# A decoder of two layers on one core: other places for the maximum products, the full-row products and the key scaling in a cross attention

## The chip, the cores and the metric

The kernel runs on one core of a Trainium2 chip. The metric is the device time in microseconds (us) of one execution. The engines are TensorE (PE: matrix products; PEld is its weight load), VectorE (DVE), ScalarE (ACT), GpSimd (POOL) and the DMA queues. They run side by side, each in its own program order, and wait for one another on semaphores. TensorE writes to PSUM, eight banks of 128 x 512 float32; the other tiles lie in SBUF.

## What is computed

A decoder of two layers, each with an attention, a cross attention and a feed-forward part. The change lies in the cross attention of layer 0, and at its seam to the recurrence that follows it. Cut to these:

```
B, S, D, HEADS, DH = 2, 1024, 256, 4, 64          # latents: 2 x 1024 tokens; context: 2 x 64 of width 192
ln = layernorm(latents); xn = layernorm(ctx)
q = ln @ Wq.T
kv = concatenate([xn @ Wkv.T, ln @ Wlkv.T], axis=1)     # 64 context keys and 1024 latent keys
q, k = rmsnorm(q) * SCALE, rmsnorm(k)                   # per head
attn = softmax(where(mask, q @ k.T, -max)); out = (attn @ v) @ Wo.T + bo
x = x + out
# recurrence over the 2 batches: f, i = sigmoid(..), g = tanh(..); c = f * c + i * g; h = tanh(x wo + c uo + bo)
x = x + ffn(layernorm(x))
```

## The kernel before

All of it is `cross_attention_and_recurrence`. The attention loop has `STEPS` = 8 steps. A step n is one batch, one half of the queries (512) and one pair of heads (`part_of`); it has `GROUPS` = 9 slots kt: eight groups of 128 latent keys, and the 64 context keys. TensorE works two slots at a time. Per slot, `scores` makes two products of 64 rows (one per head of the pair) behind two small ones that add the negative maximum ("shift"); ScalarE's `exps` takes the exponential; `values` multiplies it with V, one slot behind; GpSimd adds the slots' exponentials up in `pool_sum` (the denominator), which `add_up` sums over partitions once a step; VectorE inverts it in four quarters (`invert`) and multiplies (`normalise`).

The shift of step n+1 has to be known before its scores. For it, step n makes eight maximum products, `piece(n+1, i)` in bf16. VectorE reduces each (`reduce`), then in `split_shift` joins them in four small instructions (maximum, minimum with the context's, cast to bf16, rest); TensorE turns the result (`turn_shift`) and VectorE copies it (`keep_shift`).

One tile of two PSUM banks, `ring_tile`, holds in turn every piece, turned shift, context score (`ctx`), projection (`project`), and the mean and variance of the next layer norm. TensorE's `tile(what)` waits until VectorE has read the tile before. Which of these stand at which place is written out by hand: `tiles_at(where, slot)` with the table `PIECES_AT`. "before" stands ahead of the slot's scores, "after" behind the scores of the pair and ahead of its values. VectorE walks through the same places in its own loop and reads the tiles in the same order; between them it inverts (`INVERT_AT`), normalises, scales the queries and keys of batch 1 (`scale(1, i)`, eight tiles, in step 0) and normalises tokens. GpSimd rounds these eight tiles to bf16 (`round_tile`) at the start of step 1.

Behind the loop stand the last denominator (`add_up(7)`), the last projection, and `gate_products(b, j, m)`: three gates for each block of 512 tokens, six products each (and four with the cell's state in batch 1). The first six gates take turns in two banks, and ScalarE's `gate_values` must have read a bank before it is written again. Between them lie the layer norm of the last two token blocks (`mean`, `square`, `variance`, `roots`, `normalise_tokens`) and ScalarE's high part of the tokens, `split_x(ch)`.

Of the kernel before, what the change touches and what calls it, by code (L numbers as in the profile page):

```python
# [810 lines left out]
def cross_attention_and_recurrence(nc, c):  # L811
# [6 lines left out]
    STEPS = B * NCH * FT  # L818
# [16 lines left out]
    PIECES_AT = ((("before", 0), ("before", 1), ("after", 1), ("before", 2), ("after", 3), ("before", 4), ("after", 5), ("before", 6)),  # L835
                 (("before", 0), ("after", 0), ("before", 1), ("after", 2), ("before", 3), ("before", 4), ("before", 5), ("after", 6)))

    def tiles_at(where, slot):
        n, kt = divmod(slot, GROUPS)
        odd = n % 2  # L840
        tiles = []
        if n + 1 < STEPS:
            tiles += [("piece", n + 1, i) for i, at in enumerate(PIECES_AT[odd]) if at == (where, kt)]
        if n in (1, 2) and (where, kt) == ("before", 7):
            tiles.append(("ctx", 1, n - 1))
        if n >= 2 and not odd and (where, kt) == ("after", 7):
            tiles.append(("project", n - 1))
        if n >= 3 and odd and (where, kt) == ("after", 4):
            tiles.append(("mean", (n - 3) // 2))
        if n >= 3 and odd and (where, kt) == ("before", 7):  # L850
            tiles.append(("var", (n - 3) // 2))
        if n + 1 < STEPS and (where, kt) == ("after" if odd else "before", 8):
            tiles.append(("shift", n + 1))
        return tiles
# [3 lines left out]
    for slot in range(SLOTS):  # L858
        order += tiles_at("before", slot) + tiles_at("after", slot)
# [4 lines left out]
    with ExitStack() as ctx:  # L864
# [73 lines left out]
        QUARTERS = 4  # L938
# [31 lines left out]
        with nc.Block() as block:  # L970
# [9 lines left out]
            def _(pool):  # L980
# [20 lines left out]
                for n in range(STEPS):  # L1001
                    if n == 1:
                        pool.wait_ge(*s["scaled"](16))
                        for i in range(8):
                            round_tile(1, i)
                    if n >= 2:
                        pool.wait_ge(*s["den"](n - 1))
                    for kt in range(1, POOLED if n == STEPS - 1 else GROUPS):
                        slot = GROUPS * n + kt
# [15 lines left out]
            def _(pe):  # L1025
# [283 lines left out]
                for first in range(0, SLOTS, 2):  # L1309
# [8 lines left out]
                    for slot in range(valued, upto + 1):  # L1318
                        values(slot)
                    valued = upto + 1  # L1320
# [4 lines left out]
                add_up(STEPS - 1)  # L1325
                pe.wait_ge(*left["w", OF_TOKENS[-1]](1))
                gate_products(0, 0, 0)
                project(STEPS - 1)
                gate_products(0, 0, 1)
                pe.wait_ge(*s["read"](len(order)))  # L1330
                mean(fn, 3)
                gate_products(0, 1, 0)
                variance(fn, 3)
                gate_products(0, 1, 1)
# [18 lines left out]
            def _(act):  # L1353
# [134 lines left out]
                gate_values(0, 0, 1)  # L1488
                square(fn, 3, squares(3), fn["cent"](1))
                gate_values(0, 1, 0)  # L1490
# [15 lines left out]
            def _(dve):  # L1506
# [213 lines left out]
                def empty(what):  # L1720
# [13 lines left out]
                    else:  # L1734
                        early_norm(what)

                INVERT_AT = ({("before", 2): (0, 1), ("after", 3): (2, 3)},
                             {("before", 3): (0,), ("before", 4): (1,), ("after", 4): (2,), ("before", 5): (3,)})
                NORMALISE_AT = (("before", 4), ("before", 5))
                for slot in range(SLOTS):  # L1740
                    n, kt = divmod(slot, GROUPS)
                    for where in ("before", "after"):
                        for what in tiles_at(where, slot):
                            empty(what)
                        if n >= 1:
                            for i in INVERT_AT[n % 2].get((where, kt), ()):
                                invert(n - 1, i)
                            if NORMALISE_AT[n % 2] == (where, kt):
                                normalise(n - 1)
                    if n == 0 and kt < 8:  # L1750
                        scale(1, kt)
                    if n == STEPS - 1 and kt > POOLED + 1:
                        add(slot - 1)
                    if n == 6 and kt in (5, 7):
                        normalise_tokens(fn, kt // 2 - 2)
# [2045 lines left out]
```

## Time and profile before

| | |
|---|---|
| time, median of 3 runs | 1538.76 us (1535.29 to 1540.15) |
| the profiled execution | 1539.81 us, its span 1538.0 us |
| granted TensorE clock, mean | 0.981 |
| PE busy | 1435.8 us, 93% of the span |
| DVE, ACT, POOL busy | 984.7, 752.3, 579.7 us |
| attention loop, from the first scores to the last values | some 313 to 535 us of the span |

A row of the profile names a line of the kernel, the engine, what it writes and reads, the shape and a count. In a timeline a row begins with its start and its length, both in us; the length of several merged instructions is that of all. In brackets stands how long the engine was idle ahead of it, and whom it waited for. Times of the trace are counted from the span's start.

### The profile page before, as it was taken

To read this page: it belongs to the slowest core of one execution; us is meant where nothing else is said; L and a number is where in the kernel's file an instruction comes from. 1 tells how busy PE (TensorE), PEld (TensorE's weight loads), DVE (VectorE), ACT (ScalarE), POOL (GpSimd) and SP (SyncE) were. 2 spreads that over 40 slices of the span, in tenths; PEclk is the share of its full clock that TensorE was granted. 3 is DMA by queue.
4 is the path that set the end of the run, shared out by engine and by line. 5 is a ranking of instruction groups with operands and counts; after the bars stand their busy time and mean duration, and the time that the engine had idled before them with its cause. 6 is when DMAs were issued, how large, how long until landed. Compare 5 with 4: busy or idle time off the path is not lost. (4 is left out here: it accounts for less than half of the span.)

```text
span 1538.0 us, 19014 instructions
## 1 busy us (share of the span) xinstructions
PE 1435.8 (93%) x6886; PEld 847.3 (55%) x6886; DVE 984.7 (64%) x1502; ACT 752.3 (49%) x1237; POOL 579.7 (38%) x445
## 2 busy tenths in 40 slices
PE   6999999989899899888999999798989999999998
PEld 3757764433232266453444443323668888888886
DVE  5775243888778643558888883676677575664853
ACT  4566344533345452543666665434655545445442
POOL 0035430167667610342111112202136555555552
PEclk9999999999999999998999999999999999999999
DMA  7000000000000000083435200000313223223201
GB/s 294 1 0 0 0 1 4 0 1 1 0 0 1 1 0 0 1 164 43 125 57 70 42 2 1 4 1 7 131 42 110 76 76 101 78 81 99 74 10 55
DMA packets 39044, 67.54 MB, mean 44 GB/s; under 512 B 3944, under 2 KB 19368, under 8 KB 38568
## 3 DMA queue, kind: packets, MB, share of 16 engines
q1 hardware_dynamic: 38952, 66.33, 16.2%
q8 instruction: 55, 0.90, 0.3%
q14 instruction: 37, 0.30, 0.1%
HBM read 57.80 MB, written 8.39 MB: 43 GB/s over the span
## 5 line engine op out<-in xcount | busy, mean ns | idle before, releaser
L2289 ACT ACTIVATE arena<-psum 128x512 f32<-128x512 f32 (+1 forms) x304 | 155.2, 584 | 111.4 <-PE psum L2134 110.6
L2337 DVE TENSOR_REDUCE b_mx<-psum 128x1 f32<-128x512 f32 (+3 forms) x304 | 179.6, 650 | 45.2 <-PE psum L2112 37.1
L3081 POOL TENSOR_TENSOR m_w_rest<-m_w,m_w_high 128x512 fp32r<-128x512 f32 (+1 forms) x88 | 111.6, 1270 | 154.1 <-ACT m_w_high L3280 154.1
L3531 DVE TENSOR_TENSOR m_hidden<-m_gelu,psum 128x512 f32<-128x512 f32 (+1 forms) x88 | 60.3, 686 | 147.6 <-ACT m_gelu L3372 123.0
L3087 POOL TENSOR_TENSOR m_h_rest<-m_hidden,m_h_high 128x512 fp32r<-128x512 f32 (+1 forms) x88 | 122.3, 1389 | 59.3 <-ACT m_h_high L3294 59.3
L3174 PE MATMUL psum<-m_x_high,m_w_high 128*128 128x512 f32 (+1 forms) x352 | 137.9, 392 | 2.9 <-issue 2.9
L3174 PE MATMUL psum<-m_x_high,m_w_rest 128*128 128x512 f32 (+1 forms) x352 | 137.8, 392 | 0.0
L3174 PE MATMUL psum<-m_x_rest,m_w_high 128*128 128x512 f32 (+1 forms) x352 | 137.7, 391 | 0.0
L2032 POOL TENSOR_SCALAR_AFFINE_SELECT arena<-arena 128x512 f32<-128x512 f32 x64 | 39.9, 634 | 214.3 <-ACT arena L2289 214.3
L1014 POOL TENSOR_TENSOR x_pool_sum<-x_pool_sum,x_probs 128x1024 f32<-128x1024 f32 (+1 forms) x40 | 97.6, 2440 | 35.6 <-ACT x_probs L1384 18.4
L3372 ACT ACTIVATE m_gelu<-psum 128x512 f32<-128x512 f32 (+1 forms) x88 | 52.4, 596 | 119.0 <-PE psum L3174 119.0
L1382 ACT ACTIVATE x_probs<-psum 128x1024 f32<-128x1024 f32 x56 | 57.1, 1022 | 86.5 <-PE psum L1110 86.1
L1542 DVE TENSOR_REDUCE x_mx<-psum 128x2 f32<-128x1024 f32 x64 | 77.6, 1212 | 33.6 <-PE psum L1084 33.3
L3294 ACT ACTIVATE m_h_high<-m_hidden 128x512 fp32r<-128x512 f32 (+1 forms) x88 | 55.7, 632 | 83.0 <-DVE m_hidden L3531 83.0
L2109 PE MATMUL psum<-b_k_stack,b_q_stack 96*128 96x512 bf16 (+3 forms) x288 | 88.1, 338 | 4.4 <-DVE b_mx L2337 2.1
L2134 PE MATMUL psum<-b_q_stack,b_k_stack 98*128 98x512 bf16 (+3 forms) x288 | 83.1, 333 | 4.3 <-DMA b_q_stack<-b_stage 3.1
L3174 PEld LDWEIGHTS psum<-m_x_high,m_w_high 128*128 128x128 f32 (+1 forms) x352 | 65.5, 186 | 18.1 <-issue 3.3
L3174 PEld LDWEIGHTS psum<-m_x_rest,m_w_high 128*128 128x128 f32 (+1 forms) x352 | 65.4, 186 | 15.0
L3174 PEld LDWEIGHTS psum<-m_x_high,m_w_rest 128*128 128x128 f32 (+1 forms) x352 | 65.4, 186 | 15.0
L2149 PE MATMUL psum<-arena,weights_sb 128*32 128x512 f32 (+3 forms) x768 | 73.0, 499 | 0.0
L3187 PE MATMUL psum<-m_h_high,m_o_high 128*128 128x512 f32 (+1 forms) x176 | 72.4, 411 | 0.2 <-POOL m_h_rest L3087 0.2
L3187 PE MATMUL psum<-m_h_high,m_o_rest 128*128 128x512 f32 (+1 forms) x176 | 68.8, 391 | 0.0
(590 smaller groups left out, 3222.7 us busy)
## 6 DMA issues: line engine op xcount, KB each, us to landing
m_w<-w SPq DMA_DIRECT2D x32, 512.0 KB, 4.6
m_wo<-wo SPq DMA_DIRECT2D x16, 512.0 KB, 4.0
weights_sb<-weights SPq DMA_DIRECT2D x2, 2820.0 KB, 12.2
m_w<-w SPq DMA_DIRECT2D x16, 344.0 KB, 4.9
b_q_stack<-b_q_dram SPq DMA_DIRECT2D x36, 128.0 KB, 5.5
b_k_stack<-b_k_dram SPq DMA_DIRECT2D x36, 128.0 KB, 5.9
weights_sb<-weights SPq DMA_DIRECT2D x1, 3328.0 KB, 14.1
b_q_dram<-b_q_parts SPq DMA_DIRECT2D x6, 512.0 KB, 3.4
```

What stands on the lines that cost most here:

```text
L1014: pool.tensor_tensor(pool_sum[n % 2][rows], probs[(slot - 1) % RING][rows] if kt == 1 else pool_sum[n % 2][rows], probs[slot % RING][rows] ...
L1542: dve.tensor_reduce(mx[:, n % 2, i // 2, i % 2, :], two_heads(tile(("piece", n, i))), AX, ALU.max).then_inc(s["read"].sem)
L2109: mm = pe.matmul(bank[:, x * keys:(x + 1) * keys], qs[n % 3][0:ROWS, h, qi * P:(qi + 1) * P], ks[n % 3][0:ROWS, h, first:first + keys], st ...
L2134: mm = pe.matmul(score(i)[:, x * n:(x + 1) * n], ks[a][0:ROWS + SHIFT, h, ki * P:(ki + 1) * P], qs[a][0:ROWS + SHIFT, h, q0:q0 + n], start ...
L2149: mm = pe.matmul(out_tile[h * PAD:(h + 1) * PAD, CH - n:CH], v_aug[:, b * TT + ki, quad * QUAD + h, :], probs[(QUAD * (2 * pair + i) + h) ...
L2289: act.activation(quad_of(g)[:, heads[0]:heads[-1] + 1, 0:n], score(i)[:, 0:len(heads) * n].rearrange("p (h n) -> p h n", n=n), ACT.Exp, sc ...
L2337: dve.tensor_reduce(mx[:, part, qi, heads[0]:heads[0] + nh], tile(("piece", p))[:, 0:nh * keys].rearrange("p (h n) -> p h n", n=keys), AX, ...
L3081: pool.tensor_tensor(w_rest[:, n % W_RING, :, :, 0:H_N(n % HT)], raw_of(n), w_high[:, n % W_RING, :, :, 0:H_N(n % HT)].bitcast(F32), ALU.s ...
L3087: pool.tensor_tensor(h_rest[rows, n % H_RING, :], hidden[rows, n % 2, :], h_high[rows, n % H_RING, :].bitcast(F32), ALU.subtract).then_inc ...
L3174: mm = pe.matmul(c.bank(base + n % 2)[0:H_N(h), :], of[:, k, :], x_of[ex % 2][:, k, :], start=(k == 0 and i == 0), stop=(k == FT - 1 and i ...
L3187: mm = pe.matmul(total(m), of[rows, n % O_RING, m * P:(m + 1) * P], h_of[rows, n % H_RING, :], start=(h == 0 and i == 0), stop=(h == HT - ...
L3531: dve.tensor_tensor(hidden[rows, n % 2, :], gelu[rows, n % 2, :], c.bank(2 + n % 2)[rows, :], ALU.mult)\
```

## The change

Four places are written for each slot instead of two: "amid" stands behind the first of a pair's values, "late" behind the second. The maximum products keep away from the place between the two scores of a pair, the first of the odd steps' successors is made a step earlier, and context scores, projections, means, variances and turned shifts are moved to other places. The key scaling of batch 1 is spread over steps 0 and 1, four tiles each, and its rounding over steps 1 and 2. The four quarters of a denominator are inverted one by one. Behind the loop, the first gates stand ahead of the last `add_up`, and projection, mean and variance each one block of gates later. No instruction of the loop is added or removed but for the grouping.

```diff
-    PIECES_AT = ((("before", 0), ("before", 1), ("after", 1), ("before", 2), ("after", 3), ("before", 4), ("after", 5), ("before", 6)),
-                 (("before", 0), ("after", 0), ("before", 1), ("after", 2), ("before", 3), ("before", 4), ("before", 5), ("after", 6)))
+    WHERE = ("before", "after", "amid", "late")
+    PIECES_AT = (("early", 0), ("before", 0), ("after", 1), ("before", 2), ("after", 3), ("before", 4), ("after", 5), ("before", 6)), \
+                (("after", 0), ("before", 1), ("after", 2), ("before", 3), ("after", 4), ("before", 5), ("after", 6), ("before", 7))
...
+        if slot < 2 and where == "before":
+            tiles += [("piece", 1, slot)]
+        elif n + 1 < STEPS:
+            tiles += [("piece", n + 1, i) for i, of in enumerate(PIECES_AT[odd]) if of == at]
+        if odd and n + 2 < STEPS and at == ("after", 8):
+            tiles.append(("piece", n + 2, 0))
+        if n == 1 and at == ("amid", 6):
+            tiles.append(("ctx", 1, 0))
+        if n == 2 and at == ("after", 7):
+            tiles.append(("ctx", 1, 1))
+        if n >= 2 and not odd and at == ("before", 8):
             tiles.append(("project", n - 1))
-        if n >= 3 and odd and (where, kt) == ("after", 4):
+        if n >= 3 and odd and at == ("amid", 4):
             tiles.append(("mean", (n - 3) // 2))
-        if n >= 3 and odd and (where, kt) == ("before", 7):
+        if n >= 3 and odd and at == ("amid", 6):
             tiles.append(("var", (n - 3) // 2))
-        if n + 1 < STEPS and (where, kt) == ("after" if odd else "before", 8):
+        if n + 1 < STEPS and at == (("late", 8) if odd else ("amid", 7)):
             tiles.append(("shift", n + 1))
...
-                    if n == 1:
-                        pool.wait_ge(*s["scaled"](16))
-                        for i in range(8):
+                    if n in (1, 2):
+                        pool.wait_ge(*s["scaled"](8 + 4 * n))
+                        for i in range(4 * n - 4, 4 * n):
                             round_tile(1, i)
...
                         values(slot)
+                        for what in tiles_at("amid", second) if slot == valued else tiles_at("late", second) if slot == valued + 1 else ():
+                            fill(what)
...
-                add_up(STEPS - 1)
                 pe.wait_ge(*left["w", OF_TOKENS[-1]](1))
                 gate_products(0, 0, 0)
+                add_up(STEPS - 1)
+                gate_products(0, 0, 1)
                 project(STEPS - 1)
-                gate_products(0, 0, 1)
+                gate_products(0, 1, 0)
                 pe.wait_ge(*s["read"](len(order)))
                 mean(fn, 3)
-                gate_products(0, 1, 0)
+                gate_products(0, 1, 1)
                 variance(fn, 3)
-                gate_products(0, 1, 1)
...
+                gate_values(0, 1, 0)
                 square(fn, 3, squares(3), fn["cent"](1))
-                gate_values(0, 1, 0)
...
-                INVERT_AT = ({("before", 2): (0, 1), ("after", 3): (2, 3)},
-                             {("before", 3): (0,), ("before", 4): (1,), ("after", 4): (2,), ("before", 5): (3,)})
-                NORMALISE_AT = (("before", 4), ("before", 5))
+                INVERT_AT = ((("before", 2), ("after", 3), ("before", 4), ("after", 5)),
+                             (("before", 3), ("after", 4), ("before", 5), ("after", 6)))
...
-                    if n == 0 and kt < 8:
-                        scale(1, kt)
+                    if n <= 1 and kt in (1, 3, 5, 7):
+                        scale(1, 4 * n + kt // 2)
...
-                    if n == 6 and kt in (5, 7):
-                        normalise_tokens(fn, kt // 2 - 2)
+                    if n == 6 and kt in (7, 8):
+                        normalise_tokens(fn, kt - 7)
```

TensorE at the end of step 4, behind the scores of slots 6 and 7 (psum0 and psum3), before. L1145 is the projection of step 3, L1123 the values, L1092 the turned shift of step 5, L1105 and L1110 the scores, L1084 a maximum product:

```order
L1110 MATMUL psum3<-arena 128x512 x2
L1145 MATMUL psum1<-weights_sb 128x512 [waits x_normed,x_read]
L1145 MATMUL psum1<-weights_sb 128x512 x3
L1123 MATMUL psum2<-x_probs_last,arena 64x512 [waits x_expd]
L1123 MATMUL psum2<-x_probs_last,arena 64x512
L1123 MATMUL psum2<-x_probs0,arena 64x512 [waits x_expd]
L1123 MATMUL psum2<-x_probs0,arena 64x512
L1092 MATMUL psum1<-ident16,x_shift 128x128 [waits x_parts,x_read]
L1092 MATMUL psum1<-ident16,x_shift 128x128 x3
L1105 MATMUL psum0<-x_shift_t,x_ones16 64x512 [waits x_expd]
```

The same place after, where each of these lines has a number ten higher:

```order
L1120 MATMUL psum3<-arena 128x512 x2
L1133 MATMUL psum2<-x_probs_last,arena 64x512 [waits x_expd]
L1133 MATMUL psum2<-x_probs_last,arena 64x512
L1102 MATMUL psum1<-ident16,x_shift 128x128 [waits x_parts,x_read]
L1102 MATMUL psum1<-ident16,x_shift 128x128 x3
L1133 MATMUL psum2<-x_probs0,arena 64x512 [waits x_expd]
L1133 MATMUL psum2<-x_probs0,arena 64x512
L1155 MATMUL psum1<-weights_sb 128x512 [waits x_normed,x_read]
L1155 MATMUL psum1<-weights_sb 128x512 x3
L1115 MATMUL psum0<-x_shift_t,x_ones16 64x512 [waits x_expd]
```

The turned shift moved ahead of a slot's values and of the projection.

VectorE at the same place, before: L1574 the reciprocals, L1580 the normalisation, L1542 the reductions, L1549 to L1557 `split_shift`, L1587 and L1593 the end of the projection, L1561 the shift copy:

```order
L1574 RECIPROCAL x_den_inv<-psum2 128x128 [waits x_den] x2
L1542 TENSOR_REDUCE x_mx<-psum1 128x2 [waits x_made]
L1580 TENSOR_TENSOR weights_sb<-x_out,x_den_inv 128x512 [waits x_out_copied,x_den_inv]
L1542 TENSOR_REDUCE x_mx<-psum1 128x2 [waits x_made] x2
L1549 TENSOR_TENSOR x_top<-x_mx 128x8 [waits x_read]
L1552 SCALAR_TENSOR_TENSOR x_top<-x_top,x_mxc 128x8 [waits x_negated,x_max_step]
L1555 CAST x_shift<-x_top 128x8 [waits x_max_step]
L1557 TENSOR_TENSOR x_shift<-x_top,x_shift 128x8 [waits x_max_step]
L1587 SCALAR_TENSOR_TENSOR xT<-psum1,vectors_sb,xT 128x512 [waits x_made]
L1587 SCALAR_TENSOR_TENSOR xT<-psum1,vectors_sb,xT 128x512
L1593 TENSOR_TENSOR ln<-xT 128x512 [waits x_read]
L1561 COPY x_shift_t<-psum1 128x512 [waits x_made]
```

And after, where the numbers are twelve higher:

```order
L1586 RECIPROCAL x_den_inv<-psum2 128x128 [waits x_den]
L1554 TENSOR_REDUCE x_mx<-psum1 128x2 [waits x_made]
L1586 RECIPROCAL x_den_inv<-psum2 128x128 [waits x_den]
L1592 TENSOR_TENSOR weights_sb<-x_out,x_den_inv 128x512 [waits x_out_copied,x_den_inv]
L1554 TENSOR_REDUCE x_mx<-psum1 128x2 [waits x_made]
L1561 TENSOR_TENSOR x_top<-x_mx 128x8 [waits x_read]
L1564 SCALAR_TENSOR_TENSOR x_top<-x_top,x_mxc 128x8 [waits x_negated,x_max_step]
L1567 CAST x_shift<-x_top 128x8 [waits x_max_step]
L1569 TENSOR_TENSOR x_shift<-x_top,x_shift 128x8 [waits x_max_step]
L1573 COPY x_shift_t<-psum1 128x512 [waits x_made]
L1599 SCALAR_TENSOR_TENSOR xT<-psum1,vectors_sb,xT 128x512 [waits x_made]
```

A reciprocal and the normalisation now stand directly ahead of the last reduction, and the shift copy directly behind the split.

TensorE behind the last values, before: L1136 is `add_up(7)`, L1175 the gates, L1145 the projection:

```order
L1123 MATMUL psum2<-x_probs_last,x_v_ctx 64x512
L1136 MATMUL psum2<-x_pool_sum1,x_ones 64x512 [waits x_den_inv,x_added,x_pooled]
L1136 MATMUL psum2<-x_pool_sum1,x_ones 64x512
L1136 MATMUL psum2<-x_dve_sum,x_ones 64x512 x2
L1175 MATMUL psum0<-weights_sb_round 128x512 [waits x_expd,x_rounded]
L1175 MATMUL psum0<-weights_sb_round 128x512 x11
L1175 MATMUL psum0<-weights_sb_round 128x512 [waits f_gate]
L1175 MATMUL psum0<-weights_sb_round 128x512 x5
L1145 MATMUL psum1<-weights_sb 128x512 [waits x_normed,x_read]
```

And after:

```order
L1133 MATMUL psum2<-x_probs_last,x_v_ctx 64x512
L1185 MATMUL psum0<-weights_sb_round 128x512 [waits x_expd,x_rounded]
L1185 MATMUL psum0<-weights_sb_round 128x512 x11
L1185 MATMUL psum0<-weights_sb_round 128x512 [waits f_gate]
L1185 MATMUL psum0<-weights_sb_round 128x512 x5
L1146 MATMUL psum2<-x_pool_sum1,x_ones 64x512 [waits x_den_inv,x_added,x_pooled]
L1146 MATMUL psum2<-x_pool_sum1,x_ones 64x512
L1146 MATMUL psum2<-x_dve_sum,x_ones 64x512 x2
L1185 MATMUL psum0<-weights_sb_round 128x512 [waits f_gate]
```

The sums of the last denominator moved behind three gates, the third of which waits for ScalarE.

## Rows read from the trace of the kernel before

**Rows 1.** Windows: stretches of the loop, the seam, and one behind an idle time
```profile
core 0: us, PE busy (x) PEld busy (x) DVE busy (x) ACT busy (x) POOL busy (x), PEclk, DMA share, GB/s
...
345.29:404.06 58.77, 51.13 (x254) 17.06 (x252) 45.28 (x45) 19.78 (x21) 39.15 (x18) 0.97 0.00 1
404.06:456.68 52.62, 51.02 (x244) 16.55 (x242) 40.54 (x42) 20.62 (x22) 38.36 (x16) 1.00 0.00 1
456.68:513.77 57.09, 51.83 (x239) 16.84 (x236) 42.49 (x44) 25.22 (x27) 38.87 (x16) 0.97 0.00 1
535.28:568.03 32.75, 29.20 (x104) 18.91 (x105) 16.84 (x23) 20.71 (x26) 2.66 (x2) 0.95 0.00 1
391.00:396.00 5.00, 4.93 (x8) 2.03 (x8) 1.41 (x3) 0.00 (x0) 1.13 (x1) 0.66 0.00 0
```

**Rows 2.** Timeline of TensorE, end of step 4
```profile
442.91 0.39 PE L1084 MATMUL psum<-weights_sb 64*128 64x512 bf16 x2
...
444.21 0.38 PE L1105 MATMUL psum<-x_shift_t,x_ones 64*128 64x512 bf16 x2
...
445.38 3.70 PE L1145 MATMUL psum<-weights_sb 128*128 128x512 f32 x8
449.01 1.08 PE L1123 MATMUL psum<-x_probs_last,arena 128*64 128x512 f32 x4
...
450.88 0.40 PE L1092 MATMUL psum<-ident,x_shift 128*128 128x128 bf16 x4
```

**Rows 3.** Timeline of VectorE, end of step 4
```profile
440.58 0.93 DVE L1580 TENSOR_TENSOR weights_sb<-x_out,x_den_inv 128x512 f32<-128x512 f32 x1
...
443.35 1.22 DVE L1542 TENSOR_REDUCE x_mx<-psum 128x2 f32<-128x1024 f32 x1 [0.70 <-PE psum L1084]
444.60 1.65 DVE L1549 TENSOR_TENSOR x_top<-x_mx 128x8 f32<-128x8 f32 x1
...
446.49 2.27 DVE L1555 CAST x_shift<-x_top 128x8 bf16<-128x8 f32 x1
```

**Rows 4.** Timeline of GpSimd at the same time, two running sums
```profile
446.37 4.85 POOL L1014 TENSOR_TENSOR x_pool_sum<-x_pool_sum,x_probs 128x1024 f32<-128x1024 f32 x2
```

**Rows 5.** Timeline of VectorE: the same cast for step 0, GpSimd idle
```profile
303.27 0.18 DVE L1555 CAST x_shift<-x_top 128x8 bf16<-128x8 f32 x1
```

**Rows 6.** Timeline of TensorE: its longest waits in the loop
```profile
339.82 0.39 PE L1084 MATMUL psum<-weights_sb,x_q_guard 64*128 64x512 bf16 x2 [2.04 <-DVE x_shift_t L1561]
...
391.06 5.40 PE L1145 MATMUL psum<-weights_sb 128*128 128x512 f32 x8 [3.71 <-DVE ln L1533]
...
501.68 5.13 PE L1145 MATMUL psum<-weights_sb 128*128 128x512 f32 x8 [2.79 <-DVE x_mx L1542]
```

**Rows 7.** Timeline of TensorE at the seam
```profile
538.09 1.40 PE L1136 MATMUL psum<-x_pool_sum,x_ones 128*64 128x512 f32 x4 [2.81 <-issue]
...
541.12 3.48 PE L1175 MATMUL psum<-weights_sb_round 128*128 128x512 f32 x12
545.35 1.66 PE L1175 MATMUL psum<-weights_sb_round 128*128 128x512 f32 x6 [0.74 <-ACT arena L1416]
...
559.56 1.88 PE L1168 MATMUL psum<-x_probs,mean_w 128*128 128x512 f32 x4
```

**Rows 8.** Timeline of ScalarE at the seam
```profile
535.32 0.60 ACT L1392 ACTIVATE x_out<-psum 128x512 f32<-128x512 f32 x1 [1.76 <-PE psum L1123]
...
539.26 0.63 ACT L1407 ACTIVATE ln<-ln 128x512 f32<-128x512 f32 x1
543.32 1.28 ACT L1416 ACT_TABLE_LOAD   x1 [3.42 <-PE psum L1175]
...
547.63 1.05 ACT L1433 ACTIVATE weights_sb_round<-weights_sb 128x1024 fp32r<-128x1024 f32 x1
...
566.04 1.84 ACT L1416 ACTIVATE arena<-psum,f_bias 128x512 f32<-128x512 f32 x3
```

**Rows 9.** Timeline of VectorE at the seam: reciprocals, tokens
```profile
541.23 3.39 DVE L1574 RECIPROCAL x_den_inv<-psum 128x128 f32<-128x128 f32 x4 [3.24 <-PE psum L1136]
...
545.26 1.29 DVE L1604 TENSOR_TENSOR weights_sb<-weights_sb,ln 128x512 f32<-128x512 f32 x2
```

More of the change, by code:

```diff
@@ L840, in tiles_at @@
         odd = n % 2
+        at = where, kt
         tiles = []
[L842 to L846, printed above, removed]
+        if slot < 2 and where == "before":
[9 more added lines that the diff above has]
+        if n >= 2 and not odd and at == ("before", 8):
             tiles.append(("project", n - 1))
-        if n >= 3 and odd and (where, kt) == ("after", 4):
+        if n >= 3 and odd and at == ("amid", 4):
             tiles.append(("mean", (n - 3) // 2))
-        if n >= 3 and odd and (where, kt) == ("before", 7):
+        if n >= 3 and odd and at == ("amid", 6):
             tiles.append(("var", (n - 3) // 2))
-        if n + 1 < STEPS and (where, kt) == ("after" if odd else "before", 8):
+        if n + 1 < STEPS and at == (("late", 8) if odd else ("amid", 7)):
             tiles.append(("shift", n + 1))
@@ L858, in cross_attention_and_recurrence @@
     for slot in range(SLOTS):
-        order += tiles_at("before", slot) + tiles_at("after", slot)
+        for where in WHERE:
+            order += tiles_at(where, slot)
     order.append(("project", STEPS - 1))
@@ L1735, in empty @@
                         early_norm(what)
-                INVERT_AT = ({("before", 2): (0, 1), ("after", 3): (2, 3)},
-                             {("before", 3): (0,), ("before", 4): (1,), ("after", 4): (2,), ("before", 5): (3,)})
-                NORMALISE_AT = (("before", 4), ("before", 5))
+                INVERT_AT = ((("before", 2), ("after", 3), ("before", 4), ("after", 5)),
+                             (("before", 3), ("after", 4), ("before", 5), ("after", 6)))
                 for slot in range(SLOTS):
                     n, kt = divmod(slot, GROUPS)
-                    for where in ("before", "after"):
+                    for where in WHERE:
                         for what in tiles_at(where, slot):
                             empty(what)
[L1745 to L1748, printed above, removed]
+                        if n >= 1 and (where, kt) in INVERT_AT[n % 2]:
+                            i = INVERT_AT[n % 2].index((where, kt))
+                            invert(n - 1, i)
+                            if i == QUARTERS - 1:
                                 normalise(n - 1)
-                    if n == 0 and kt < 8:
-                        scale(1, kt)
+                    if n <= 1 and kt in (1, 3, 5, 7):
+                        scale(1, 4 * n + kt // 2)
                     if n == STEPS - 1 and kt > POOLED + 1:
                         add(slot - 1)
-                    if n == 6 and kt in (5, 7):
-                        normalise_tokens(fn, kt // 2 - 2)
+                    if n == 6 and kt in (7, 8):
+                        normalise_tokens(fn, kt - 7)
                 add(SLOTS - 1)
```

## The prediction

> **What bounds the kernel now.** I read the page first, then the windows over the attention loop, then the rows of each engine there. The loop has eight steps of nine slots. TensorE paces it: between slot 1 of step 3 and slot 1 of step 5 it is busy for 51.02 of 52.62 us [rows 1], and ScalarE, VectorE and GpSimd have room. So what the change can give or take are TensorE's waits. Few are left: 1.6 us in steps 3 and 4, but 5.3 in steps 5 and 6, 7.6 in steps 1 and 2, 3.6 at the seam to the recurrence [rows 1]. In the rows TensorE waits for one thing above all, the single ring tile (two banks of PSUM) through which every maximum product, turned shift, projection and mean passes, and which VectorE must have read before the next is made.
>
> Two behaviours price a wait. First, VectorE's small steps of `split_shift`. In step 0 the cast takes 0.18 us [rows 5]; in step 4 the first step takes 1.65 and the cast 2.27 [rows 3], and both end as one of GpSimd's running sums ends, which follow each other every 2.5 us [rows 4]. So between the last reduction's end and a finished shift lie 4.4 us when GpSimd works (444.60 to 448.99, from the first step's start to 0.2 after the cast) and about 0.8 when it doesn't. Second, a long idle time of TensorE costs twice: behind 3.71 and 2.79 us of idle time the eight projection products take 5.40 and 5.13 us [rows 6] against 3.70 [rows 2]; the granted clock there is 0.66 [rows 1], part of the stretch at 1.2 GHz, not 2.4. That is 1.4 to 1.7 us more for each wait of about 3 us.
>
> The Trainium skill has the first as a rule (SBUF — State Buffer, "Who interferes with whom"): an instruction of VectorE with two SBUF inputs, or a cast in a two-port mode, and GpSimd's exclude each other for a whole instruction. By that rule the length of a split is a matter of what GpSimd does at that moment, which this case's rows bear out at 0.18 and 2.27 us for one instruction; the rival "free split" below is what it would make of the time where GpSimd is idle.
>
> **The change, part by part.** *Even steps: the shift is turned two places earlier.* Before, the order behind the last maximum product is two scores, projection, two values, shift; after, two scores, one value, shift, one value, projection. Cover before: 450.88 - 442.91 = 7.97 us [rows 2], and the shift did not wait. Cover after: that less the projection (3.63) and one value (0.94, from 449.01 to 450.88 for two), so 3.4 us. What must fit: product to reduction 0.44 us (442.91 to 443.35), reduction 1.25, split 4.4, 0.1 to the start. That is 6.2 us. The last quarter of the reciprocals and the normalisation (0.93, [rows 3]) now stand directly ahead of this reduction, where before the normalisation came one product earlier; walking VectorE's queue through the three pairs of slots with reductions of 1.15, reciprocals of 0.85 (3.39 for four, [rows 9]) and the normalisation of 0.9, the reduction starts 0.9 later. It may also find GpSimd in another phase of its 2.5 us; I take 0.5 off for that. Taken: 6.6 needed, 3.4 covered, a wait of 3.2 us, plus 1.6 for the clock: 4.8 us in each of steps 2, 4 and 6. Behind the waiting shift stand the projection and all scores; ScalarE and GpSimd run dry later.
> - Step 4 had no such wait: +4.8.
> - Step 2: the projection waited 3.71 there and lost 1.7 of clock [rows 6]. VectorE's chain (split, then the context maximum, which now stands ahead of the shift) is the same: +0.
> - Step 6: the wait of 2.79 and the 1.4 behind it [rows 6] came from a token normalisation ahead of the last reduction; it moves behind the shift and off the path: 4.8 - 4.2 = +0.6. The two roots on ScalarE at the end of step 5 then hold back the first exponentials of a step that starts earlier: +1.0, estimated.
>
> *Odd steps: the last maximum product comes one pair later, a product of the next step follows, the shift comes behind two values.* Cover: product, two scores, product, two values, 4.6 us; needed 2.4 if the split is short, 6.6 if not, and the next product's reduction behind it adds 1.2. By the walk GpSimd's sixth sum ends about 0.7 us before the split, and the seventh's exponential comes 0.4 us after it: no wait in steps 3 and 5. Bounds 0 to 4.8 each; I take 0. The early product saves the waits of product on product at the start of even steps and one 0.25 behind: -1.1 per pair of steps. Steps 3 and 4 together: 4.8 - 1.1 = +3.7. Steps 5 and 6: 0.6 + 1.0 - 1.1 = +0.5.
>
> *Key scaling over two steps.* Each scaling reads two SBUF tiles and so meets GpSimd. Four leave step 0, where two of them stood ahead of the shift copy; where the next step's first product now waits 2.04 us for that copy, with a slow clock behind it [rows 6], it would wait for nothing, and the turned shift waits some 3 us instead of 2: about 3 us gained by slot 1 of step 1, by the walk. The four that go to step 1 stand ahead of reductions, and the last stands directly between the split and the next product's reduction, on which the shift now waits: up to 2.5 us and another 2.5 if the split meets GpSimd. Taken: -3.1 and +5.1, so +2.0 up to the end of step 2; bounds -4 and +7, the one if the split of step 1 is short, the other if it is long and every scaling waits. The four roundings that GpSimd does a step later are needed in step 3: nothing. No transfer is moved.
>
> *Fewer changes of array shape.* A scores pair takes 1.17 us ahead of a full-row product (444.21 to 445.38) and, with the product's 0.23 taken off 442.91 to 444.21, 1.07 ahead of scores [rows 2]: 0.1 per change of shape, at most 3 a step, up to 2 us in all, of which most merely moves. Taken: 0. The Trainium skill (TensorEngine Tiling (Array Packing), "Key Properties") says that a change of tiling mode drains TensorE; the row agrees, at 0.1 us.
>
> *The seam.* Before: idle 2.81, sums of the last denominator, first gates [rows 7]. After: the first three gates, then the sums. Let X be the end of the last values, 535.3. The third gate needs bank 0 back from ScalarE, which first copies out, does two roots with their table loads and loads the sigmoid's table: 539.26 + 0.63 is X+4.6, and from the start of that load to the third gate are 2.03 us (543.32 to 545.35): X+6.7 [rows 7, 8]. TensorE runs two gates (2.8 us) and idles 3.9. Then third gate 1.4, sums 1.9, clock 1.7: the denominator is ready at X+11.7, before at 541.12, X+5.8. Reciprocals 3.39, normalisation and tokens 0.6 + 1.3 [rows 9]: ScalarE's split of the third token block, which stood at X+12.3 [rows 8] and did not hold anything up, starts at X+17.2 and ends at X+18.2. It stands ahead of the next gate values in ScalarE's order; the first of these, which TensorE's sixth gate waits for, is there at X+19.0. TensorE reached that gate at X+14.5: a wait of 4.5 us and 1.7 of clock. From there sixth gate 1.4, projection 3.0, three gates 4.2, mean 1.0, three gates 4.2 bring the variance to X+34.5. Before, three gates stood behind the variance and covered the two roots (559.56 to 566.04 and the first gate value, 7.2 us [rows 7, 8]); now only one gate of 3.1 us and the variance's 1.3 do: the second gate of the next block starts at X+41.7, after 32.75 before [rows 1]. +9.0, and 1.4 of clock: +10.4. Bounds: +3.5 if the split's delay were covered, +12.
>
> **Sum.** 2.0 + 3.7 + 0.5 + 10.4 = +16.6, and everything behind the layer waits for it: the page's chain of waits runs over TensorE, and from 535.28 to 568.03 and on it has next to no slack. The profiled execution took 1539.8 us (its span 1538.0) and would take 1556.4; the median of the runs is 1.05 below it, so 1555.
>
> **Rivals.**
> *Only the loop loses* (1543 to 1548). If the third token block's split were not late, the seam would give about +4 or less. For it: TensorE and ScalarE both idle there today, 2.81 and 3.42 us [rows 7, 8]. Against: the orders of both engines are fixed, and I see no path around the third gate's wait.
> *Only the seam loses* (1547 to 1551). Odd and even splits both meet GpSimd lightly.
> *Free split, faster* (about 1530). If GpSimd were idle at the splits, each 4.4 us would be 0.8 [rows 3, 5]: the waits of steps 0, 1, 2, 4 and 6 with their clock, 4.5 + 6.3 + 4.8 + 4.8 + 4.8 = 25 us in my walk, would go, and 16.6 - 25 = -8 would remain, the seam's loss within it. It decides from four of these five steps on. Against: in step 4 GpSimd runs sum behind sum from slot 2 to slot 7 [rows 4], as its input is ready early.
> *Nothing to be seen* (1534 to 1543): ring waits only change places.
>
> **How the numbers follow.** Both lose, as summed: 0.60. Only the seam 0.13, only the loop 0.09, nothing 0.07, faster 0.11. A change under 0.3% (4.6 us) can't be told from none. Slower: 0.60 + 0.13 + 0.09 and a little of the fourth, 0.83; same 0.07; faster 0.10. The range takes both slower rivals and the upper bounds of step 1 and the odd steps: 1543 to 1565.
>
> **What would show it.** Right: a wait of about 3 us ahead of the turned shift in steps 2, 4, 6, with a granted clock near 0.7 behind; the cast there at 2.27 us and near 0.2 in steps 3 and 5; gates idle 4 us twice ahead of the last projection and 3 behind the last variance. Wrong: a cast that is short in even steps, or the third token block's split before X+14.

## The result, and the profile after

The changed kernel takes 1554.72 us (median of 4 runs, 1546.57 to 1556.23) where the kernel before took 1537.03 beside it (4 runs). The ratio is 1.0107, interval 1.0061 to 1.0153: slower by about 1.1%. Its profiled execution has a span of 1552.0 us against 1538.0. The forecast was 1555 in 1543 to 1565.

The stages first. The windows below cut the loop where the prediction cut it, at slot 1 of a step; the first starts at the first product of step 1's maxima. The columns are those of [rows 1].

Kernel before, the stretches that [rows 1] does not have alone:
```profile
313.17:345.29 32.12, 25.29 (x124) 7.75 (x125) 27.99 (x23) 10.43 (x11) 23.76 (x15) 0.95 0.00 1
345.29:370.75 25.46, 22.41 (x122) 7.50 (x120) 21.14 (x20) 9.77 (x11) 20.10 (x10) 1.00 0.00 1
370.75:404.06 33.31, 28.73 (x134) 9.55 (x132) 24.13 (x25) 10.01 (x11) 19.05 (x8) 0.95 0.00 0
```
Kernel after, all stretches; the last is the seam, from the end of the last values to the second gate of the second sequence:
```profile
311.79:339.18 27.39, 23.31 (x120) 7.29 (x122) 20.96 (x18) 10.43 (x11) 19.31 (x9) 1.00 0.00 1
339.18:370.52 31.34, 24.60 (x124) 7.95 (x122) 25.70 (x26) 9.35 (x10) 24.57 (x17) 0.93 0.00 1
370.52:404.09 33.57, 30.20 (x132) 10.04 (x130) 21.59 (x23) 10.43 (x11) 19.04 (x8) 0.86 0.00 0
404.09:461.81 57.72, 53.75 (x245) 17.31 (x243) 37.47 (x42) 20.62 (x22) 38.22 (x17) 0.94 0.00 1
461.81:519.48 57.67, 52.18 (x240) 16.87 (x237) 40.78 (x45) 25.22 (x27) 37.81 (x17) 0.97 0.00 1
519.48:541.34 21.86, 21.78 (x96) 6.54 (x94) 13.65 (x11) 13.56 (x16) 18.73 (x10) 1.00 0.01 1
541.34:583.47 42.13, 32.61 (x106) 20.26 (x104) 16.51 (x23) 19.68 (x24) 2.36 (x1) 0.88 0.00 0
```
The first column is the length, the next TensorE's busy time, the seventh its granted clock. Steps 3 and 4 have the same work as in [rows 1] (x245 against x244), but TensorE is busy for 2.7 us more, at a clock of 0.94 instead of 1.00, and idle for 2.4 us more. That is the two-fold price of a wait. The loss lies in three places: step 1 (5.9 us, against which step 0 gains 4.7), steps 3 and 4 (5.1), and the seam (9.4).

TensorE's waits for the turned shift (line 1102, before 1092), one row each for steps 0, 1, 2, 4 and 6, and what follows in step 4:
```profile
333.03 0.38 PE L1102 MATMUL psum<-ident,x_shift 128*128 128x128 bf16 x4 [2.53 <-DVE x_shift L1569]
...
365.90 0.40 PE L1102 MATMUL psum<-ident,x_shift 128*128 128x128 bf16 x4 [4.43 <-DVE x_mx L1554]
...
391.73 0.61 PE L1102 MATMUL psum<-ident,x_shift 128*128 128x128 bf16 x4 [3.31 <-DVE ln L1545]
...
449.15 0.58 PE L1102 MATMUL psum<-ident,x_shift 128*128 128x128 bf16 x4 [2.97 <-DVE x_shift L1569]
449.67 1.98 PE L1133 MATMUL psum<-x_probs,arena 128*64 128x512 f32 x4
451.58 5.47 PE L1155 MATMUL psum<-weights_sb 128*128 128x512 f32 x8
...
508.46 0.38 PE L1102 MATMUL psum<-ident,x_shift 128*128 128x128 bf16 x4 [2.98 <-DVE x_shift L1569]
```
Before, the shift of step 4 did not wait, one value took 0.94 and the projection 3.70 [rows 2]. VectorE's side of it, the cast of step 3 and three rows of step 4, and then GpSimd, the sum nearest to that cast of step 3 and three sums of step 4:
```profile
424.96 0.19 DVE L1567 CAST x_shift<-x_top 128x8 bf16<-128x8 f32 x1
...
445.21 1.07 DVE L1561 TENSOR_TENSOR x_top<-x_mx 128x8 f32<-128x8 f32 x1
446.32 0.17 DVE L1564 SCALAR_TENSOR_TENSOR x_top<-x_top,x_mxc 128x8 f32<-128x8 f32 x1
446.52 2.26 DVE L1567 CAST x_shift<-x_top 128x8 bf16<-128x8 f32 x1
```
```profile
425.48 2.35 POOL L1024 TENSOR_TENSOR x_pool_sum<-x_pool_sum,x_probs 128x1024 f32<-128x1024 f32 x1 [1.80 <-ACT x_probs L1394]
...
443.64 2.62 POOL L1024 TENSOR_TENSOR x_pool_sum<-x_pool_sum,x_probs_last 128x1024 f32<-128x1024 f32 x1
446.40 4.83 POOL L1024 TENSOR_TENSOR x_pool_sum<-x_pool_sum,x_probs 128x1024 f32<-128x1024 f32 x2
```
The first step ends 0.02 us after the sum that started at 443.64 (446.28 against 446.26), the cast as the next sum ends. The cast handles 8 columns and takes 2.26 us. In step 3 GpSimd stands idle for 1.80 us up to 425.48, and the cast inside that time takes 0.19, as forecast.

The seam, TensorE and then ScalarE (they answer to [rows 7, 8]):
```profile
548.09 2.93 PE L1185 MATMUL psum<-weights_sb_round 128*128 128x512 f32 x6 [3.74 <-ACT arena L1428]
550.95 1.98 PE L1146 MATMUL psum<-x_pool_sum,x_ones 128*64 128x512 f32 x4
...
561.55 2.93 PE L1185 MATMUL psum<-weights_sb_round 128*128 128x512 f32 x6 [4.15 <-ACT arena L1428]
...
583.47 1.65 PE L1185 MATMUL psum<-weights_sb_round 128*128 128x512 f32 x6 [1.64 <-ACT arena L1428]
```
```profile
559.87 1.06 ACT L1445 ACTIVATE weights_sb_round<-weights_sb 128x1024 fp32r<-128x1024 f32 x1 [8.12 <-DVE weights_sb L1616]
```
With X = 541.34 the third gate starts at X+6.8 (forecast 6.7), ScalarE's split of the third token block at X+18.5 (17.2), the sixth gate at X+20.2 after a wait of 4.15 (19.0 after 4.5).

### The profile page after: what moved, and what is told of

It reads as the page before. It is cut to its first block and busy times, and to the rows that moved or that the text cites. A ratio compares the mean times of both kernels' runs of the same rounds, so it can differ in the third digit from the quotient of the medians.

```text
span 1552.0 us, 19014 instructions
## 1 busy us (share of the span) xinstructions
PE 1441.1 (93%) x6886; PEld 848.9 (55%) x6886; DVE 977.0 (63%) x1502; ACT 752.3 (48%) x1237; POOL 578.1 (37%) x445
```

## The experiments

Theory: the loss has two homes that add up, the seam's order and the even steps' shift; the second is only paid because GpSimd's running sums stretch VectorE's small steps. Rivals: only one of the two; VectorE's own queue makes the shift late; ring waits just change places. Kernels of one group (the first four of the table, the next four, the last three) ran on one chip beside the kernel before, whose medians there were 1538.31, 1537.11 and 1536.93 us. The changed kernel was not run again in these groups: where a median is held against its 1554.72, up to 1.4 us can be the difference of the groups, and the ratios are the safer measure.

| kernel | median us | ratio to before, 95% |
|---|---|---|
| seam_of_before | 1548.13 | 1.0062 (1.0040 to 1.0084) |
| even_shift_back | 1547.62 | 1.0069 (1.0052 to 1.0087) |
| narrow_sums | 1538.92 | 1.0014 (1.0001 to 1.0027) |
| late_scaling | 1552.65 | 1.0104 (1.0083 to 1.0125) |
| hold_sums | 1531.71 | 0.9966 (0.9953 to 0.9979) |
| hold_sums_seam_of_before | 1525.07 | 0.9918 (0.9903 to 0.9933) |
| hold_in_before | 1532.88 | 0.9974 (0.9959 to 0.9989) |
| sums_first | 1545.21 | 1.0053 (1.0038 to 1.0068) |
| only_new_seam | 1546.55 | 1.0065 (1.0044 to 1.0085) |
| odd_steps_and_scaling | 1534.42 | 0.9995 (0.9976 to 1.0015) |
| two_gates_first | 1521.83 | 0.9905 (0.9885 to 0.9925) |

**seam_of_before**: TensorE's calls behind the loop as before, and ScalarE's square ahead of the gate values.
```diff
+add_up(STEPS - 1)
 gate_products(0, 0, 0)
-add_up(STEPS - 1)
-gate_products(0, 0, 1)
 project(STEPS - 1)
-gate_products(0, 1, 0)
+gate_products(0, 0, 1)
...
```


> The changed kernel with the orders of TensorE and ScalarE at the seam as they were before. My account: from the end of the last values to the second gate of the second sequence 42.1 us go back to 32.8, and everything up to there stays; 1544.5 us, ratio to the kernel before about 1.005. Rival (only the loop loses): that stretch falls by under 4 us and the time stays at 1551 or more. Rival (only the seam loses): the time comes down to that of the kernel before, 1537 to 1540.

From slot 1 of step 7 to the second gate of the second sequence the changed kernel needs 63.99 us (the last two windows above), this one 52.98:
```profile
518.49:571.47 52.98, 49.41 (x201) 24.95 (x199) 30.36 (x34) 34.25 (x42) 21.09 (x11) 1.00 0.00 1
```
So the stretch goes back by 11.0 us and neither rival holds. That is 1.3 us below the 54.26 of the kernel before, though the orders at the seam are the same: its idle time of 2.73 us ahead of the last denominator's sums had no slow clock behind it (1.00 over the stretch, against 0.97). The median falls by less, 6.6 us, to 1548.13 where 1544.5 was expected, in a kernel whose runs spread from 1537.4 to 1551.2.

**even_shift_back**: for even steps the projection at the place ("after", 7), the shift at ("before", 8).
```diff
-if n >= 2 and not odd and at == ("before", 8):
+if n >= 2 and not odd and at == ("after", 7):
     tiles.append(("project", n - 1))
-if n + 1 < STEPS and at == (("late", 8) if odd else ("amid", 7)):
+if n + 1 < STEPS and at == (("late", 8) if odd else ("before", 8)):
```


> The changed kernel with the turned shift of the even steps back behind the projection and two values (projection ahead of them, as before); odd steps, scaling and seam stay as changed. My account: the waits of 2.97 and 2.98 us in steps 4 and 6 go with their slow clock, so slot 1 of step 3 to slot 1 of step 5 falls from 57.7 to about 53 and the next two steps by as much; in step 2 the wait of 3.31 only moves to the projection. About -9.5 us against the changed kernel, 1545. Rival (ring waits only change places): the projection waits instead, the two stretches stay within 1.5 us and the time at 1552 or more.

Steps 3 and 4, then 5 and 6:
```profile
404.61:456.39 51.78, 50.74 (x244) 16.51 (x242) 38.05 (x42) 20.62 (x22) 38.26 (x17) 1.00 0.00 1
456.39:510.46 54.07, 50.44 (x240) 16.31 (x238) 41.28 (x45) 25.23 (x27) 38.52 (x17) 1.00 0.00 1
```
57.72 falls to 51.78 and 57.67 to 54.07: 9.5 us as expected. Step 2 gains nothing: its projection waits 4.31 and then takes 6.36, and steps 1 and 2 together take 65.85 us against 64.91. The median is 7.1 below the changed kernel's. Both stretches also lie below the kernel before (52.62 and 57.09 in [rows 1]), by 0.8 and 3.0 us. These come from what is left of the change there: the odd steps' orders, the reciprocals one by one and, in step 6, the later token normalisation. No run tells them apart.

**narrow_sums**: what GpSimd does during the split, taken away.
```diff
+wide = slice(0, 8 if n in (2, 4, 6) and kt in (4, 5, 6, 7) else CH)
```


> The changed kernel, but GpSimd's running sums of key groups 4 to 7 in steps 2, 4 and 6 take 8 of each head's 512/2 columns (the other columns of these groups are left out of the denominator), so GpSimd is nearly idle at the even splits. If GpSimd's sums stretch the split: the cast of 2.26 us falls to 0.2, the first step of 1.07 to 0.2, the wait for the turned shift goes from 2.97 to under 0.5 in steps 4 and 6 and by 2 or more in step 2, with the slow clock behind; about -4.5 us a step, -13 in all, 1541 to 1543. Rival (VectorE's queue, the last reciprocals and the normalisation directly ahead of the reduction, makes the shift late): cast and wait stay as they are or the wait falls by under 1 us a step; 1552 or more.

Of the 512 columns of each head's sum, 8 are left in those groups; the addition takes the columns `wide` of its three operands. VectorE in step 4, then TensorE:
```profile
438.67 1.22 DVE L1556 TENSOR_REDUCE x_mx<-psum 128x2 f32<-128x1024 f32 x1
439.92 0.17 DVE L1563 TENSOR_TENSOR x_top<-x_mx 128x8 f32<-128x8 f32 x1
440.12 0.17 DVE L1566 SCALAR_TENSOR_TENSOR x_top<-x_top,x_mxc 128x8 f32<-128x8 f32 x1
440.32 0.25 DVE L1569 CAST x_shift<-x_top 128x8 bf16<-128x8 f32 x1
```
```profile
441.17 0.40 PE L1104 MATMUL psum<-ident,x_shift 128*128 128x128 bf16 x4
...
442.51 3.70 PE L1157 MATMUL psum<-weights_sb 128*128 128x512 f32 x8
```
The last reciprocal and the normalisation still stand directly ahead of the reduction, and the wait is gone: VectorE's queue was not the cause. The steps fall by 5.2 (1 and 2), 5.9 (3 and 4) and 4.7 us (5 and 6), 15.8 in all, and so does the median (1554.72 to 1538.92). That is more than the 13 expected, and 1538.92 lies below the 1541 to 1543. The Trainium skill (SBUF — State Buffer, "Who interferes with whom") has the rule that an instruction of VectorE with two SBUF inputs, or one in a two-port mode, and GpSimd's exclude each other for a whole instruction; 2.26 against 0.25 us for one cast agree with it.

**late_scaling**: the fourth scaling of step 1 behind the copy of the turned shift.
```diff
-if n <= 1 and kt in (1, 3, 5, 7):
-    scale(1, 4 * n + kt // 2)
+if n <= 1 and kt in ((1, 3, 5, 8) if n else (1, 3, 5, 7)):
+    scale(1, 4 * n + min(kt // 2, 3))
```


> The changed kernel with the last of step 1's four key scalings behind the copy of the turned shift instead of ahead of the reduction that the shift waits for. My account: the wait of 4.43 us in step 1 falls by the scaling and what it waits for GpSimd, to about 2, and the slow clock behind it goes: -3.5 us, 1551. Rival (the split itself is long there): the wait stays above 3.5 and the time at 1554 or more.

The rival was right about the wait, which falls from 4.43 to 3.82 only:
```profile
366.76 0.61 PE L1102 MATMUL psum<-ident,x_shift 128*128 128x128 bf16 x4 [3.82 <-DVE x_mx L1554]
```
The median falls by 2.1, within the spread, and 1552.65 lies between the two forecasts. Steps 1 and 2 together take 62.52 us instead of 64.91; of these 2.4 us the wait is 0.6, the rest is TensorE's busy time (53.02 against 54.80), with less of the slow clock. In the changed kernel, step 1, VectorE and GpSimd:
```profile
359.40 2.23 DVE L1564 SCALAR_TENSOR_TENSOR x_top<-x_top,x_mxc 128x8 f32<-128x8 f32 x1
...
361.88 2.25 DVE L1569 TENSOR_TENSOR x_shift<-x_top,x_shift 128x8 bf16<-128x8 f32 x1
364.03 0.68 DVE L1535 SCALAR_TENSOR_TENSOR arena<-ln,arena 128x512 f32<-128x512 f32 x1
```
```profile
359.25 2.35 POOL L1024 TENSOR_TENSOR x_pool_sum<-x_pool_sum,x_probs 128x1024 f32<-128x1024 f32 x1 [1.59 <-ACT x_probs L1394]
361.74 2.33 POOL L1024 TENSOR_TENSOR x_pool_sum<-x_pool_sum,x_probs_last 64x1024 f32<-64x1024 f32 x1
```
Two of the split's four steps meet one sum each and take 4.1 us more than the 0.2 that each takes alone; the scaling itself finds GpSimd free and takes 0.68.

**hold_sums**: nothing left out; GpSimd merely yields.
```diff
 pool.wait_ge(*s["expd"](slot + 1))
+if n + 1 < STEPS and kt == (7 if n % 2 else 5):
+    pool.wait_ge(*s["parts"](n + 2))
```


> The changed kernel, complete in its output, in which GpSimd waits in each of steps 0 to 6 ahead of one running sum (the fifth group's in even steps, the seventh's in odd ones) until VectorE has finished the split of the shift. If GpSimd at the split is the cause: every split takes about 0.8 us, the waits of 2.53, 4.43, 3.31, 2.97 and 2.98 for the turned shift go under 0.7 with the slow clock behind them; -16 as in narrow_sums for steps 2, 4, 6, -5 for step 1, -3 for step 0: 1531. Rival (the sums held back are late for the denominators at slot 1 of the next step or for ScalarE's ring of exponentials): new waits there give back more than half, 1543 or more.

GpSimd, VectorE and TensorE in step 4:
```profile
434.02 2.35 POOL L1026 TENSOR_TENSOR x_pool_sum<-x_pool_sum,x_probs_last 128x1024 f32<-128x1024 f32 x1 [2.67 <-DVE x_shift L1571]
436.51 7.61 POOL L1026 TENSOR_TENSOR x_pool_sum<-x_pool_sum,x_probs 128x1024 f32<-128x1024 f32 x3
446.27 2.36 POOL L1026 TENSOR_TENSOR x_pool_sum<-x_probs 128x1024 f32<-128x1024 f32 x1 [2.15 <-ACT x_probs L1396]
```
```profile
433.47 0.19 DVE L1569 CAST x_shift<-x_top 128x8 bf16<-128x8 f32 x1
```
```profile
434.03 0.38 PE L1104 MATMUL psum<-ident,x_shift 128*128 128x128 bf16 x4
```
The cast takes 0.19 us. GpSimd gives up 2.67 us, has caught up by the next step's first sum (at 446.27 it waits for ScalarE again), and the turned shift no longer waits. Steps 1 and 2 take 56.69 us instead of 64.91, 3 and 4 51.87, 5 and 6 53.02; the seam is as slow as before the edit (63.93 against 63.99). The median is 1531.71 us, 1531 was expected. The rival's new waits, for denominators or for exponentials, are not there; the longest wait left in the loop is one of 2.07 us in step 1.

**hold_sums_seam_of_before**: that edit and that of seam_of_before.

> The same with the seam's orders of before. If loop and seam add up: -7 to -10 more than hold_sums, 1521 to 1524, below the kernel before by about 1%. Rival (the loss of the seam hangs on how late the loop's last sums are): less than 3 us below hold_sums.

It is 6.6 us below hold_sums and ends at 1525.07, both a little short of the forecast; the stretch from slot 1 of step 7 to the second gate falls by 9.3 us (63.93 to 54.63). Loop and seam add up, and this version is faster than both kernels.

**hold_in_before**: the same hold in the kernel before (groups 5 and 6).

> The kernel before with the same kind of hold (the fifth group's sum in even steps, the sixth's in odd ones). It keeps its orders, whose even shift has cover for 4.4 us of split: only its waits of steps 0, 1 and 2 can shrink, about -6 us, 1531. If the new orders of the loop are worth something once the split is short, hold_sums_seam_of_before is 5 us or more below this one. Rival (any order profits alike): within 3 us of each other.

It is 4.2 us below the kernel before beside it, where 6 was expected, and 7.8 above hold_sums_seam_of_before. The splits are short here too, but there are new waits for the shift copy, one of 1.37 us in step 4 and this one in step 6 (TensorE, then VectorE):
```profile
503.34 0.61 PE L1107 MATMUL psum<-x_shift_t,x_ones 64*128 64x512 bf16 x2 [5.20 <-DVE x_shift_t L1563]
```
```profile
496.23 1.22 DVE L1595 TENSOR_TENSOR ln<-xT 128x512 f32<-128x512 f32 x1
497.37 2.83 DVE L1606 TENSOR_TENSOR weights_sb<-weights_sb,ln 128x512 f32<-128x512 f32 x1
```
In the order of before, the sums of the projected halves and a token normalisation stand between split and shift copy, and now it is they that meet the sums GpSimd catches up with (the second row is one of two such instructions). So steps 5 and 6 take 59.82 us, longer than before (57.09), and steps 3 and 4 54.03, against 53.02 and 51.87 in hold_sums; steps 1 and 2 take 54.38, less than its 56.69. The changed order, which turns and copies the shift right behind the split, can use a short split: its loss in even steps comes from meeting long splits, not from the order alone. How much of the 7.8 us is that order's is not shown, since the two kernels also differ in the token normalisation, the scaling and the odd steps.

**sums_first**: the changed kernel with `add_up(STEPS - 1)` ahead of the first gates, all else kept.

> The changed kernel with the sums of the last denominator ahead of the first three gates as before, the rest of the seam as changed. My account: the wait of 4.15 us for the third token block's split goes with its slow clock, the shorter cover of the last roots stays: from the end of the last values to the second gate of the second sequence 36 instead of 42.1, 1548.5. Rival (the roots' cover is the larger part): less than 3 us gained, 1552 or more.

```profile
519.25:575.83 56.58, 51.37 (x201) 25.29 (x199) 30.18 (x33) 33.27 (x40) 21.13 (x11) 0.97 0.00 1
```
From 63.99 to 56.58: 7.4 us for the late denominator. The rest of the seam's loss, 56.58 against 54.26 in the kernel before, is mostly the wait of 1.64 behind the last variance. The median fell by 9.5, to 1545.21 where 1548.5 was expected.

**only_new_seam**: the kernel before with the changed seam alone.

> The kernel before with nothing but the changed orders of TensorE and ScalarE at the seam. My account: from the end of the last values to the second gate of the second sequence 42 us instead of 32.8, the loop untouched: +9.4, 1546.5. Rival (the seam's loss needs the changed loop): under +3.

From slot 1 of step 7 to the second gate:
```profile
512.22:576.20 63.98, 54.50 (x201) 26.72 (x199) 30.14 (x32) 33.25 (x40) 21.43 (x11) 0.92 0.00 1
```
It is the same 64 us as in the changed kernel, with the waits 3.69, 4.14 and 1.64, and the median is 9.6 us above the kernel before beside it. The seam's loss needs nothing of the new loop.

**odd_steps_and_scaling**: the edits of seam_of_before and even_shift_back together.

> The changed kernel with both other parts put back: the seam as before, and the turned shift of the even steps behind the projection. Left of the change are the odd steps and the scaling. From the two single runs (-6.6 and -7.1 against the changed kernel, each with some 2 us of spread) 1540 to 1541; by my own terms (+2.0 for scaling, -1.1 for each pair of steps) 1538 to 1540. Rival (odd steps or scaling cost on their own): 1545 or more.

The median is 1534.42, the ratio 0.9995 (0.9976 to 1.0015): not told from the kernel before, and better than the 1540 from the two single runs. The part of the change that is left may be worth up to 0.24% or cost up to 0.15%.

**two_gates_first**: hold_sums_seam_of_before, with the seam's idle time filled. `gate_products` takes which of its three gates to make.
```diff
-add_up(STEPS - 1)
-gate_products(0, 0, 0)
+gate_products(0, 0, 0, (0, 1))
+add_up(STEPS - 1)
+gate_products(0, 0, 0, (2,))
+gate_products(0, 0, 1, (0,))
 project(STEPS - 1)
-gate_products(0, 0, 1)
+gate_products(0, 0, 1, (1, 2))
...
```


> hold_sums_seam_of_before (1525.07) with TensorE's idle time of 2.73 us at the seam filled: the first two gates ahead of the sums of the last denominator, which stay where they are in time since they wait for VectorE's last running sum; third and fourth gate before the projection. The second gate of the second sequence 2.7 to 2.9 us earlier: 1522. Rival (the third gate waits for ScalarE's copy, roots and table loads as in the changed kernel, and what is gained is waited there): within 1 us of 1525.

```profile
520.14 3.06 PE L1187 MATMUL psum<-weights_sb_round 128*128 128x512 f32 x12
523.13 1.08 PE L1148 MATMUL psum<-x_pool_sum,x_ones 128*64 128x512 f32 x4
524.04 1.03 PE L1148 MATMUL psum<-x_dve_sum,x_ones 128*64 128x512 f32 x4
526.89 4.61 PE L1187 MATMUL psum<-weights_sb_round 128*128 128x512 f32 x12 [1.83 <-ACT arena L1433]
```
Each account is half right: two gates now cover the wait for VectorE's last sum, and 1.83 us are waited behind it for ScalarE's copy, two roots and table loads. The stretch from slot 1 of step 7 to the second gate falls from 54.63 to 52.88. The median of 1521.83 is the lowest of all versions and what was expected, 0.9905 of the kernel before. But it ran on another chip than hold_sums_seam_of_before, and the two intervals overlap, so that it is faster than that one rests on the 1.75 us of the traces alone.

## Why the prediction was right, step by step

| term | forecast | measured in the trace |
|---|---|---|
| up to slot 1 of step 1 | -3.1 | 32.12 to 27.39: -4.7 |
| from there to slot 1 of step 2 | +5.1 | 25.46 to 31.34: +5.9 |
| step 2 | 0 | 33.31 to 33.57: +0.3 |
| steps 3 and 4 | +3.7 | 52.62 to 57.72: +5.1 |
| steps 5 and 6 | +0.5 | 57.09 to 57.67: +0.6 |
| seam | +10.4 | 32.75 to 42.13: +9.4 |
| all (of the unrounded times) | +16.6 | +16.5 |

The slots between the last two rows took 0.35 more (21.86 against 21.51). The span grew by 14.0 only, since the stage starts 1.4 us earlier (311.79 against 313.17) and the rest of the program is shorter by about as much. The start is no part of the account: over all these kernels it lies between 309.5 and 314.8 us.

The causes were the ones forecast, but that the sum came out to 0.1 us, and the median to 0.3, is partly luck. Single terms were off by 1.6 us and less on either side and cancelled, and the changed kernel's own runs spread over 9.7 us.

*The seam* is the best supported: its three waits came at their places (3.9, 4.5 and 3 forecast, 3.74, 4.15 and 1.64 measured), and it was shown apart in three ways (out of the changed kernel, into the kernel before, and with its first half alone). Two sizes were off and cancelled: the split of the third token block came 1.3 us later, since the third gate and the sums behind the first wait took 6.3 us at the slow clock (548.09 to 554.39) where 5.0 were forecast; and the third wait was half as long, with no slow clock behind it.

*Even steps.* The wait was 2.97 against 3.2. The clock's term, 1.6, was too small where it was paid: it came from the projection alone ([rows 6] against [rows 2]), but in steps 2 and 4 the value ahead of the projection slows too. In step 4 the shift to the next scores takes 7.83 us at a clock of 0.62, and 4.95 at 1.00 in seam_of_before, 2.9 us for one wait. That is most of the missing 1.4 of steps 3 and 4. In step 6 it was 1.7 (508.46 to 515.09, 6.63 us), near the forecast. The premise that the split takes 4.4 us because of GpSimd, and the rival that follows from it, are both borne out by narrow_sums and hold_sums. The forecast priced five free splits at 25 us; hold_sums gave 23.0.

*Odd steps.* The splits of steps 3 and 5 are short, nothing waits there, and the early product may save what was said: steps 3 and 4 of even_shift_back are 0.8 below the kernel before, with the whole of the odd steps' orders and the single reciprocals in them, where 1.1 was forecast for the product.

*Scaling.* Step 0 gained 1.6 us more than forecast (4.7 against 3.1), with its clock at 1.00 instead of 0.95. The sum for step 1 was near (5.9 against 5.1), but its cause was misplaced. The forecast put the scaling that stands "directly between the split and the next product's reduction" first, at up to 2.5 us. In late_scaling it is worth 0.6 us of the wait. The larger share is the split itself, 4.9 us from the start of its first step to the end of its last (359.20 to 364.13), the possibility that I had named second.

*Array shape*, taken 0: no experiment isolates it.

Not settled: how the medians divide. Even steps are worth 7.1 us by even_shift_back against the changed kernel, but 13.7 by odd_steps_and_scaling against seam_of_before; the seam 6.6 to 13.2 in the same way. All four compare medians of different groups, which can make up 1.4 us of each. The stretches of the traces give 9.5 less the 0.9 lost in steps 1 and 2, and for the seam 9.3 to 11.0. The likely reason is the clock, below, but no run varies it alone.

## What to carry over

Before moving a step earlier, look at what its producer shares with a third engine at that moment: a VectorE step of 8 columns cost as much as GpSimd's instruction of 1024, and one wait a step on GpSimd, which had room, was worth 23 us of 1555. Work moved ahead to fill a wait should not hold up the start of a chain over other engines: three gates moved ahead of a denominator cost about 7 us at the far end. Filling the idle time with no more than fits (two gates, not three) kept the chain and took 1.75 us off the stretch.

## What the hardware showed that was not expected

The same idle time does not always bring the slow clock. The shift of step 4 waits 2.96 or 2.97 us in three kernels; behind it the projection takes 5.47 us in the changed kernel and 3.70 in seam_of_before and late_scaling:
```profile
449.15:456.98 7.83, 7.83 (x18) 2.71 (x18) 0.42 (x1) 0.00 (x0) 2.08 (x1) 0.62 0.00 0
```
```profile
451.15:456.10 4.95, 4.95 (x16) 1.84 (x17) 0.42 (x1) 0.00 (x0) 2.06 (x1) 1.00 0.00 0
```
In both the engine had been granted 1.00, its 2.4 GHz, over the 16 us up to the wait; behind it stands 1.2 GHz for most of the first stretch and for none of the second. The work around the wait is the same in all three, only the time at which it comes differs, as far as the profile shows. The kernel before and only_new_seam, whose loops are the same code, show it too: behind the same wait of 2.79 us in step 6 the projection takes 5.13 us in one and 3.70 in the other. The changed kernel's own four runs fit: one took 1546.57 at a mean clock of 0.978, the others 1553.68 to 1556.23 at 0.971 to 0.973. Whether the number of such waits sets the spread is not shown: the changed kernel spread by 9.7 us, and hold_sums, whose loop has no wait over 2.1 us, by 2.2, but sums_first keeps the loop's waits of 2.5 to 4.4 us and spread by 2.6, each of these two over five runs only.
